# Expert biases added by VectorE from a bank spread over the partitions, in place of bias products in the tiles of a Flamingo layer with a routed expert FFN

## What is computed

```python
shared = silu(x @ sh_up_w + sh_up_b) @ sh_down_w + sh_down_b
scores = softmax(xf @ gate_w.T)                 # 8 experts
topk_w, topk_i = top_k(scores, 2)
topk_w = topk_w / topk_w.sum()
h = silu(einsum('nd,edh->neh', xf, up_w) + up_b)        # up_b: (8, 256)
ye = einsum('neh,ehd->ned', h, down_w) + down_b         # down_b: (8, 256)
y = einsum('ned,ne->nd', ye, comb)
x = x + tanh(g_ffn) * (y + shared)
```

## Time and profile before

| | us |
|---|---|
| runs, median of 3 | 622.09 |
| lowest, highest | 621.01, 624.24 |
| the profiled execution | 620.84 |
| its span | 619.0 |
| busy: PE, VectorE, ACT, POOL | 528.8, 431.5, 333.1, 267.7 |
| first gather of an expert tile issued | 495.0 |
| last product of PE | about 594 |
| last addition issued by POOL | 608.1 |

### The profile page before, as it was taken

One profiled execution on the slowest core, in us unless ns is written; L12 is line 12 of the kernel. 1 busy time (PEld: TensorE's weight loads), 2 busy tenths in 40 slices (PEclk: granted clock), 3 DMA queues, 4 the chain that ended last, 5 costly groups with the idle time before them and its releaser, 6 DMA issues.

```text
span 619.0 us, 13953 instructions
## 1 busy us (share of the span) xinstructions
PE 528.8 (85%) x3944; PEld 496.0 (80%) x3945; DVE 431.5 (70%) x1247; ACT 333.1 (54%) x1091; POOL 267.7 (43%) x276
## 2 busy tenths in 40 slices
PE   1789999988989998898999889899976969999940
PEld 1678989888979897897989789798965868999930
DVE  7768877778768777876877787677758874555520
ACT  2477656646755665575567556546755814444410
POOL 3357525324433433443243334325357305565663
PEclk9889999999999999999999999989988979999985
DMA  4551300000100000000000000000955345676753
GB/s 146 167 170 41 120 11 20 28 1 18 35 0 0 27 26 0 18 18 17 0 27 26 0 9 27 0 0 29 318 165 167 106 145 96 106 112 114 102 59 37
DMA packets 42580, 38.81 MB, mean 63 GB/s; under 512 B 9907, under 2 KB 41076, under 8 KB 42548
## 3 DMA queue, kind: packets, MB, share of 16 engines
q1 hardware_dynamic: 34684, 28.16, 15.2%
q0 software_dynamic: 7536, 10.27, 9.5%
q10 hardware_dynamic: 330, 0.02, 0.0%
HBM read 19.51 MB, written 18.93 MB: 62 GB/s over the span
## 4 chain that ended last, share of the span: by engine, by line
PE 49%; DVE 20%; issue 12%; ACT 10%; POOL 4%; DMA 2%; DVEq 1%; SPq 0%; POOLq 0%; ACTq 0%
PE bank L1436 15%; PE bank L1438 13%; PE bank L1437 13%; ACT norm_probs L747 5%; PE bank L1653 2%; DVE acts L1117 2%; PE bank L1596 2%; POOL norm_probs L582 2%; DVE acts L1045 2%; ACT acts L729 2%; POOL acts L587 1%; ACT acts L722 1%; DVE nmax L1074 1%; PE bank L1742 1%; PE bank L1748 1%
## 5 line engine op out<-in xcount | busy, mean ns | idle before, releaser
L582 POOL TENSOR_TENSOR norm_probs<-norm_probs,rden 128x512 f32<-128x512 f32 x64 | 66.3, 1036 | 144.5 <-DVE rden L1108 144.4
L1436 PE MATMUL bank<-acts,weights 128*128 128x256 f32 x384 | 109.8, 286 | 3.0 <-DVE weights L986 2.9
L1437 PE MATMUL bank<-acts,weights 128*128 128x256 f32 x384 | 108.9, 284 | 0.0
L1438 PE MATMUL bank<-acts,weights 128*128 128x256 f32 x384 | 108.8, 283 | 0.0
L747 ACT ACTIVATE norm_probs<-bank,nmax 128x128 f32<-128x128 f32 x256 | 90.5, 366 | 33.6 <-DVE nmax L1074 32.5
L1436 PE MATMUL bank<-weights,acts 128*128 128x256 f32 x256 | 80.2, 313 | 21.7 <-DVE acts L1045 14.8
L587 POOL TENSOR_TENSOR acts<-uf,acts 128x256 fp32r<-128x256 f32 x64 | 47.4, 740 | 99.1 <-ACT acts L739 99.1
L675 POOL DMA_INDIRECT out_x<-norm_probs,th x39 | 60.6, 1555 | 56.5 <-DVE norm_probs L1427 24.7
L739 ACT ACTIVATE acts<-uf 128x256 fp32r<-128x256 f32 x64 | 26.7, 418 | 100.7 <-DVE uf L1144 100.6
L1436 PEld LDWEIGHTS bank<-acts,weights 128*128 128x128 f32 x384 | 73.4, 191 | 6.1 <-issue 3.5
L1045 DVE TENSOR_TENSOR acts<-bank,acts 64x256 fp32r<-64x256 f32 x128 | 53.9, 421 | 32.4 <-ACT acts L722 31.6
(11 more groups left out here) (239 smaller groups left out, 1541.4 us busy)
## 6 DMA issues: line engine op xcount, KB each, us to landing
slot_rows<-tf SPq DMA_DIRECT2D x8, 680.0 KB, 5.8
spare<-slot_rows SPq DMA_DIRECT2D x39, 128.0 KB
ct<-in_ctx SPq DMA_DIRECT2D x8, 256.0 KB, 2.7
xs<-in_x SPq DMA_DIRECT2D x8, 256.0 KB, 5.2
spare<-in_L_xattn_Wff SPq DMA_DIRECT2D x8, 256.0 KB, 4.4
out_x<-xs SPq DMA_DIRECT2D x4, 512.0 KB, 3.0
stage<-in_L_ffn_up_w SPq DMA_DIRECT2D x5, 256.0 KB, 2.8
stage<-in_L_ffn_down_w SPq DMA_DIRECT2D x5, 256.0 KB, 3.1
```

Of the source, the lines that this page charges most:

```text
L582: pool.tensor_tensor(pr[:, s % 2], pr[:, s % 2], rden[:, s % 2, :].unsqueeze(2).broadcast_to((P, 4, P)), ALU.mult).then_inc(probs_ready, 1)
L1436: pe.matmul(ps, wts[1], mov[0], start=first, stop=False, skip_group_check=True)
L1437: pe.matmul(ps, wts[0], mov[0], start=False, stop=False, skip_group_check=True)
L1438: return pe.matmul(ps, wts[0], mov[1], start=False, stop=last, skip_group_check=True)
```

## The change

The biases of all experts are loaded spread over the 128 partitions into a bank, `bias_all`: for each expert 256 values of `up_b` and 256 of `down_b`. It lies over a buffer for weights (`slow_stage`, moved in front of `xs`) and over the first three of the four stored groups of `xs`. `add_bias` and `brow` leave the tiles. VectorE now adds the bias to the up product out of PSUM into `biased` (SBUF), from which ACT makes the SiLU; it adds the bias to the down product into `ys`, and ACT multiplies that in place with the tokens' weights. VectorE reads the expert numbers of four tiles from a table (`value_load`) and works out the address of the bias in registers.

```diff
@@ -143,3 +143,4 @@
 
-        xs = sb("xs", [P, NB, D])
+        xs_t = sb("xs", [P, 1024 + NB * D])
+        slow_stage, xs = xs_t[:, 0:1024], xs_t[:, 1024:].rearrange("p (b n) -> p b n", n=D)
         ct = sb("ct", [P, 2, D])
@@ -174,5 +175,4 @@
         xmT = [xmT_t[:, 0:KT], xmT_t[:, KT:2 * KT]]
-        spare = sb("spare", [P, 4 * ROW + 8 + 1024])
+        spare = sb("spare", [P, 4 * ROW + 8])
         xrow, xrow_last = [spare[:, 2 * ROW * i:2 * ROW * (i + 1)].rearrange("p (t n) -> p t n", t=2) for i in range(2)]
-        slow_stage = spare[:, 4 * ROW + 8:]
         rows_g = spare[:, 0:4 * D].rearrange("p (s n) -> p s n", s=4)
@@ -219,3 +219,5 @@
 
-        shared_brow, brow = acts[:, 0:D], acts[:, D:D + 2 * NE * D]
+        shared_brow = acts[:, 0:D]
+        bias_all = xs_t[:, 0:2 * NE * D]
+        biased = [u1, uf]
         consts = tf.rearrange("p k n -> p (k n)")
@@ -325,3 +327,5 @@
         shared_brow_in = sem("shared_brow_in")
-        brow_in = sem("brow_in")
+        bias_in = sem("bias_in")
+        tile_biased = sem("tile_biased")
+        y_biased = sem("y_biased")
         tables_done = sem("tables_done")
@@ -373,2 +377,11 @@
 
+        def weighted(eng, t, loop):
+
+            if isinstance(t, int):
+                at = ((t - 2) % RING) * D
+                return meta[:, t - 2, 1:2], slice(at, at + D)
+            i, j = loop
+            return (meta[:, bass.ds(i * WINDOW + j, 1), 1:2].rearrange("p a n -> p (a n)"),
+                    bass.ds(eng.snap((i & 1) * (WINDOW * D) + j * D), D))
+
         def chunk_split(n):
@@ -489,7 +502,13 @@
             sp.wait_ge(wo_done, NG * NU)
-            for a in range(2):
-                sp.dma_start(brow[a:a + 1, :].bitcast(F32),
-                             bias_rows[a, 0:2 * NE].rearrange("(o r) d -> o (r d)", o=1)).then_inc(brow_in, 16)
             load_chunk(NCA + 8)
 
+            def load_biases(n):
+
+                for i, b in enumerate((up_b, down_b)):
+                    sp.dma_start(bias_all[:, 1024 * n:1024 * n + 1024].rearrange("p (e i d) -> p e i d", e=2, i=2)[:, :, i],
+                                 b[2 * n:2 * n + 2].unsqueeze(0).broadcast_to((P, 2, D))).then_inc(bias_in, 16)
+
+            split(sp, NCA + 5)
+            load_biases(0)
+
             def store_tiles(j):
@@ -512,3 +531,6 @@
             pairs_by_tile = by_tile[:, :, D:ROW].rearrange("a p (e k) -> a p e k", k=2)
-            store_tiles(0)
+            for j in range(TPS - 1):
+                store_tiles(j)
+                sp.wait_ge(written, 16 * j + 16)
+                load_biases(j + 1)
             sp.wait_ge(tables_done, 1)
@@ -517,4 +539,3 @@
                 load_tile(t, t)
-            for j in range(1, TPS):
-                store_tiles(j)
+            store_tiles(TPS - 1)
             for t in range(4, 7):
@@ -859,6 +880,6 @@
                 if runs(t):
-                    act.wait_ge(tile_up_filled, t + 1)
+                    act.wait_ge(tile_biased, t + 1)
                     if not (isinstance(t, int) and t < 2):
                         act.wait_ge(hT_filled, t - 1)
-                    act.activation(hs[:, c % 2, :], bank[2 + c % 2][:, 0:HID], ACT.Silu).then_inc(tile_silu_done, 1)
+                    act.activation(hs[:, c % 2, :], biased[c % 2][:, :], ACT.Silu).then_inc(tile_silu_done, 1)
                 if runs(t + 2):
@@ -873,2 +894,6 @@
                                    ).then_inc(hTh_done, 1)
+                if runs(t - 2):
+                    weight, y_at = weighted(act, t, loop)
+                    act.wait_ge(y_biased, t - 1)
+                    act.activation(ys[:, y_at], ys[:, y_at], ACT.Copy, scale=weight).then_inc(y_copied, 1)
 
@@ -1402,3 +1427,21 @@
 
+            experts_of = None
+
             def tile_step(t, c, loop):
+                nonlocal experts_of
+
+                k = loop[1] if loop else t - 2 if t < 2 else (t - 2) % WINDOW
+                if t == 0 if loop is None and t < WINDOW else k == 0:
+                    w = loop[0] if loop else max(t - 2, 0) // WINDOW
+                    if loop is None and t == 0:
+                        dve.wait_ge(tables_done, 2)
+                        dve.wait_ge(bias_in, 16 * 8)
+                    experts_of = dve.value_load(window[0:1, bass.ds(w, 1)])
+                if runs(t):
+                    e = dve.snap((experts_of >> (SHIFT * (k + 2))) & (NE - 1))
+                    dve.wait_ge(tile_up_filled, t + 1)
+                    if not (isinstance(t, int) and t < 2):
+                        dve.wait_ge(tile_silu_done, t - 1)
+                    dve.tensor_tensor(biased[c % 2][:, :], bank[2 + c % 2][:, 0:HID], bias_all[:, bass.ds(e * 2 * D, D)], ALU.add
+                                      ).then_inc(tile_biased, 1)
                 if runs(t + 2):
@@ -1412,17 +1455,13 @@
                 if runs(t - 2):
+                    e = dve.snap((experts_of >> (SHIFT * k)) & (NE - 1))
+                    _, y_at = weighted(dve, t, loop)
+                    if not isinstance(t, int):
+                        dve.wait_ge(y_added[loop[1]], loop[0] * 16)
+                    elif t - 2 >= RING:
+                        dve.wait_ge(y_added[(t - 2) % 4], 16 * ((t - 2) // 4))
+                    elif t - 2 == RING // 2 - 1:
+                        dve.wait_ge(ring_ready, NPOS)
                     dve.wait_ge(tile_down_filled, t - 1)
-                    b = (c + 2) % 4
-                    if isinstance(t, int):
-                        n, weight = t - 2, meta[:, t - 2, 1:2]
-                        y_at = slice((n % RING) * D, (n % RING) * D + D)
-                        if n >= RING:
-                            dve.wait_ge(y_added[n % 4], 16 * (n // 4))
-                        elif n == RING // 2 - 1:
-                            dve.wait_ge(ring_ready, NPOS)
-                    else:
-                        i, j = loop
-                        weight = meta[:, bass.ds(i * WINDOW + j, 1), 1:2].rearrange("p a n -> p (a n)")
-                        y_at = bass.ds(dve.snap((i & 1) * (WINDOW * D) + j * D), D)
-                        dve.wait_ge(y_added[j], i * 16)
-                    dve.tensor_scalar(ys[:, y_at], bank[6 + c % 2][:, 0:D], weight, None, ALU.mult).then_inc(y_copied, 1)
+                    dve.tensor_tensor(ys[:, y_at], bank[6 + c % 2][:, 0:D], bias_all[:, bass.ds(e * 2 * D + D, D)], ALU.add
+                                      ).then_inc(y_biased, 1)
 
@@ -1650,6 +1689,5 @@
 
-            def add_bias(b, row):
+            def add_bias(b):
 
-                pe.matmul(b, pick, shared_brow if row is None else brow[:, bass.ds(row, D)], start=True, stop=False,
-                          skip_group_check=True)
+                pe.matmul(b, pick, shared_brow, start=True, stop=False, skip_group_check=True)
 
@@ -1672,3 +1710,3 @@
                         t = 2 * pair + i
-                        add_bias(b[:, i * D:(i + 1) * D], None)
+                        add_bias(b[:, i * D:(i + 1) * D])
                         for k in range(KT):
@@ -1717,3 +1755,2 @@
                         split(pe, NCA + 1 + n)
-                    pe.wait_ge(brow_in, 32)
                     pe.wait_ge(tables_done, 2)
@@ -1730,7 +1767,8 @@
                     b = bank[2 + c % 2][:, 0:HID]
+                    if not (isinstance(t, int) and t < 2):
+                        pe.wait_ge(tile_biased, t - 1)
                     pe.wait_ge(xg_ready, t + 1)
-                    add_bias(b, e * D)
                     for kt in range(KT):
                         done = matmul3(b, [x[:, c % 2, kt, :] for x in xg], [expert_w(e)(a, kt, 0, HID) for a in range(2)],
-                                       False, kt == KT - 1)
+                                       kt == 0, kt == KT - 1)
                     done.then_inc(tile_up_filled, 1)
@@ -1754,7 +1792,6 @@
                     if not (isinstance(t, int) and t < 4):
-                        pe.wait_ge(y_copied, t - 3)
-                    add_bias(b, e * D + NE * D)
+                        pe.wait_ge(y_biased, t - 3)
                     for kt in range(KT):
                         done = matmul3(b, [x[c % 2][:, kt, :] for x in hsT],
-                                       [expert_w(e)(2 + a, kt, 0, D) for a in range(2)], False, kt == KT - 1)
+                                       [expert_w(e)(2 + a, kt, 0, D) for a in range(2)], kt == 0, kt == KT - 1)
                     done.then_inc(tile_down_filled, 1)
```

## The result

The change makes the kernel slower: 641.28 us median of 4 runs (639.14 to 645.36) against 621.99 of 4 (621.01 to 624.24), ratio 1.0313 with a 95% interval of 1.0248 to 1.0378, +19.3 us. The forecast was 633.9 with a range of 628 to 640, so the time lies above the range. The direction holds, and so do the two causes that the forecast named, the late start and the slower loop; the late start was priced too low.

A forecast was written before the change was run, and what follows sets the result against it. POOL's chain of additions, 2.54 us per tile, was taken to set the end, not PE. Tile 4 8.0 us late and a ring of 2.68 us per tile made tile 30 11.8 late: 622.09 + 11.8 = 633.9 us, range 628 to 640.

The forecast's parts named there:

- the late start: Start of the expert stage: gathers wait on SP behind stores and bias loads, so tile 4 is about 8.0 us late.
- the slower loop: Expert tile loop: VectorE and ACT, tied into a ring, need 2.68 us per tile, above POOL's 2.54.
- The bias bank, SP's queue: SP before the gathers: bias loads wait for stores landing in 3.0 us, making gather 4 8.0 us late.
- POOL's chain sets the end, PE does not: Expert stage: from tile 4 on POOL's additions, 2.54 us per tile, set the end; PE only sets their start.
- Tile 4, +8.0: First added tiles: 8.0 late, less 0.35 of PE, plus 0.45 behind the products; ready at 531.2 instead of 523.2.
- The ring, 2.68 us per tile: Loop: VectorE and ACT wait on each other in turn; 2.16 plus 0.52 of registers, bounds 2.16 and 2.85.
- ACT's weighting copy: Loop, ACT: the 39 new copies with the tokens' weights cost nothing, by 0.1 us.
- The registers: Loop, VectorE: register work lies between the instructions and hides nothing; 2.07 us per four steps, 0.52 per step.
- The bare ring of 2.16: Loop: once round VectorE's and ACT's instructions, with all registers hidden, takes 2.16 us; the lower bound.
- Registers under instructions: Loop, VectorE: whether register work runs under the add ahead; forecast said no. If so, POOL decides, 630.1; chance 0.27.
- Tile 4 to tile 30, +3.8: POOL's stretch between these additions: grows from +8.0 at tile 4 to +11.8 at tile 30.
- slower than the bounds: Rival, loop: idle PE is granted a clock of 0.50 for long, about 650 us; slower than 640 had chance 0.04.

The follow-up runs named there:

- e1: Kernel before the change without the two bias products of each expert tile: 623.72 us against 621.39, ratio 1.0018.
- e2: Kernel before, with the change's SP order, stores 0 to 2 each awaited until landed before the first gather, no bias loads: 628.94 us, ratio 1.0122.
- e10: Kernel before with the changed kernel's whole SP order, bias loads included but the bank unread: 635.16 us, ratio 1.0166.
- e3: Changed kernel with a bank of only one pair of experts' biases and SP's order as before: 628.28 us, ratio 1.0114.
- e4: e3 without ACT's weighting copies, POOL adding the tile as VectorE's bias add leaves it: 624.55 us, ratio 1.0042.
- e7: e3 with VectorE's bias rows at a fixed address, so no table word loaded and no row computed: 625.91 us, ratio 1.0023.
- e5: Changed kernel with stores ahead of bias pairs on SP, each pair awaiting its own store, gathers still last: 637.65 us, ratio 1.0240.
- the half bank: Against the kernel before: only up biases added by VectorE, from a half-size bank; down biases stay PE products, weights VectorE's: 626.91 us, ratio 1.0047.
- e8: Changed kernel with POOL issuing the bias loads and their waits for landed stores, SP's order as before: 636.64 us, ratio 1.0240.

## Why the prediction was wrong, and where it was right

The step that failed is the term "The bias bank, SP's queue": it let a store land in 3.0 us with two loads of biases ahead of it, and took from that 8.0 us for the late start.

- **POOL's chain sets the end, PE does not: right.** e1 takes 1.67 of 20 us of PE's work in the stage away (19.87 to 18.20) and gains nothing. The Trainium skill (page "Perfetto Trace Analysis", section "Identifying the Most-Contended Engine") would have PE as the engine to relieve, with weight loads busy for 19.47 of 20 us; e1 and the result speak against it here. (The forecast's 9.1 us for the products lie between its own 39 x 0.23 = 9.0 and 78 x 0.12 = 9.4; nothing hangs on that.) (The forecast's 9.1 us for the products lie between its own 39 x 0.23 = 9.0 and 78 x 0.12 = 9.4; nothing hangs on that.)
- **"The bias bank, SP's queue": the term that failed.** It said 8.0 us for gather 4, from stores that land in 3.0 us and from sums that hold store 2 back. Measured from R: 10.6. The waits with their 3.0 us are worth 6.3 (e2), a bit less than forecast; on top come 3.9 us (e10) for something that was not in the sum at all: each store stands behind a pair of loads, 512 KB, and lands in 5.4 to 6.2 us. That costs twice, at store 1, whose landing lets store 2 go 1.2 us after its sums, and at store 2. The earlier trace rows had its price only for stores with no such loads ahead, and the upper bound of 4.1 was the maximum of the same four.
- **"Tile 4, +8.0": wrong by the same, and by the ring.** From R it is 12.2. Behind gather 4 the forecast added 0.1 us. Measured from gather 4 to the addition of tile 4: 16.8 us before, 16.9 in e10 with the loop of before, 18.3 in the changed kernel and 18.5 in e3. So 1.6 us are the changed loop's, in its first tiles. The prediction let the ring begin at tile 4.
- **The ring, 2.68 us per tile: right by number, not by parts.** Measured 10.9 / 4 = 2.7. Two terms were off and cancelled. ACT's weighting copy, "cost nothing, by 0.1 us", costs 0.20 to 0.25 in three steps of four, 0.66 in the four (10.9 against 10.24 in e4), 0.17 per tile. It starts 0.65 us after the y bias and not 0.54, SiLU follows 0.41 later and not 0.28 (the copy takes 0.51 us, not the 0.42 of the earlier trace rows), and the up bias ends at 0.74 and not at 0.92. The registers were 0.52 per step in the sum. Those that e7 leaves out cost about 0.9 / 4 = 0.24 per tile; it keeps the ring's address and the loop's branch. In e4 all that four tiles take over four bare steps is 10.24 - 4 x 2.18 = 1.52, 0.38 per tile, 1.27 of the 1.52 at the top. The bare ring of 2.16 was right: e4's inner step is 2.18. So 2.18 + 0.38 + 0.17 = 2.73.
- **Registers under instructions.** In the last step of the four y bias and up bias are 0.33 apart with three register instructions between them (541.15 and 541.48), no more than L1406 to L1410 in the earlier trace rows. There the Trainium skill's rule (the same page, section "Sequencer Loop") holds, and the prediction set it aside for all steps. Where more stand between two adds, a little shows: 0.45 (536.10 to 536.55) and 0.49 (535.61 to 536.10), much as the 0.46 of the earlier trace rows. At the top of the loop the rule does not hold: 1.32, and 0.70 without the table's word and the rows.
- **Tile 4 to tile 30, +3.8: right.** 69.84 - 65.95 = 3.9. The same for the tail: tile 30 to the end 28.6 us against 28.4. The 4.47 of the earlier trace rows for a new expert was the shortest of the seven in that trace, which take up to 5.19.
- **What carried the time out of the range.** Of the 19.3 us 11.8 were forecast. The late start adds 4.2, the rest of the chain 0.2. That alone would make 638.3, inside the range. 2.05 us ahead of R are in the profiled span of after, and the profiled execution of after lies 2.14 us under its median, that of before 1.15 under its own; these 3 us are not assigned to a cause. The rival "slower than the bounds" had the right sign and the wrong reason: in the stretch 560 to 580 the granted clock is 1.00.

The sum with the measured terms, from R: waits 6.5, loads 3.9, ring in the first tiles 1.8, ring from tile 4 to 30 3.9, together 16.1. The 1.8 are what 12.2 leaves over e10's 10.4, so they are no measurement of their own; gather 4 to tile 4 gives 1.6 for them.

## What to carry to other kernels

Before costing work saved on the busiest engine, follow the chain of the last output step: here POOL's indirect additions, at 2.54 us per tile, hid 9 us of PE work, and any engine that needs more than 2.54 costs time. A transfer's time to land must be taken with what will stand ahead of it, not from a row in which it ran alone, above all where a wait hangs on it and other work queues behind the wait. And where space is reused, the first use waits for the part of the space that is freed last: four orders of the same loads gained no more than some 3 us of the 11 by which the first add was late against e7, though e5's trace leaves room for an earlier one than any of them reached; the half bank, whose space was free early, kept the first gather within 2.5 us of before.

## What the runs showed of the hardware that was not expected

- A 512 KB store that lands in 3.0 us without loads (e2) took 5.3 to 5.7 behind two 256 KB loads in the same queue (e10; 5.4 to 6.2 in the changed kernel), 3.1 to 3.3 ahead of them (e5), and up to 5.6 with the loads in POOL's queue (e8). Another queue did not shield it.
- ACT's copy with a scale read from SBUF took 0.510 us for 128x256, against 0.418 for a plain copy of that shape:

```profile
L898 ACT ACTIVATE norm_probs<-norm_probs,th x39: 507/510/512, 526.3 to 623.5; - x28, 128x256 f32<-128x256 f32 x11
```

- POOL's indirect additions followed each other by 1.85 to 1.87 us in every trace wherever the tile was ready and the expert the same, whatever the other engines did; in the changed kernel one landed in 3.8 to 4.3 us. Where an addition had to wait until the last one had landed, it followed by 4.4 to 6.0 us.
- Loads reach further than their own queue. In e3 no wait for a store stands ahead of the first gather, and yet it came at 29.7 us from R instead of 27.7. The tables were done at the same moment (VectorE's row for them starts at 493.79, before at 493.85), but POOL's scattered rows, which the gathers wait for too, landed later once pair 0 was loaded beside them. Landing of POOL's scatters between 478 and 500, in the kernel before and in e3:

```profile
DMA to landing us min/median/max: 2.4/2.6/3.4
```

```profile
DMA to landing us min/median/max: 2.5/5.0/5.5
```

The last scatter was issued at 491.27 and at 491.31 and landed in 2.7 and in 4.9 us, at 494.0 and 496.2; the gather went out at 495.00 and 497.08. Where POOL issued the pairs after its scatters (e8) the first gather was at 27.5.
